# A graph network on one core: counts of two target rows kept in one float32 value, and two layers that unpack them and multiply exact parts in single-pass products, a block at a time

## The reference, cut to what matters

```python
def _L0_gnn_ref(feature, edge_src, edge_dst, W1, b1, W2, b2):
    msgs = feature[edge_src]
    neigh = jax.ops.segment_sum(msgs, edge_dst, num_segments=N_NODES)
    h = (1.0 + EPS) * feature + neigh
    h = jax.nn.relu(h @ W1 + b1)
    return h @ W2 + b2
...
def _L2_gnn_ref(x, edge_index, w_self, b_self, w_neigh, b_neigh):
    agg = jax.ops.segment_sum(x[src], dst, num_segments=n)
    deg = jnp.maximum(deg, 1.0)[:, None]
    mean_neigh = agg / deg
    return x @ w_self.T + b_self + mean_neigh @ w_neigh.T + b_neigh
...
h = relu(layernorm(x)); x = x + _L0_gnn_ref(h, src, dst, ...)
h = relu(layernorm(x)); x = x + _L1_gnn_ref(h, edge_attr_64, ...)   # attention over edges
h = relu(layernorm(x)); x = x + _L2_gnn_ref(h, edge_index, ...)
h = relu(layernorm(x)); x = x + _L3_gnn_ref(h, src, dst, edge_weight, ...)
```

## Time and profile before

| | |
|---|---|
| median of 3 timed runs | 5309.13 us (5304.78 to 5313.57) |
| profiled execution, its own time | 5340.31 us |
| its span in the trace | 5338.3 us |
| mean granted PE clock | 0.927 |
| busy: PE, DVE, ACT, POOL | 4369.5, 3074.2, 1790.3, 2045.5 us |

### The profile page before, as it was taken

The page is one execution under the profiler, slowest core; times in us unless marked ns, Lnnn a source line. Parts: engine busy times, 40 slices in busy tenths (PEclk is TensorE's granted clock), DMA queues, the critical chain, the costliest instruction groups (busy, mean ns, idle before and its releaser), DMA issues. The chain is left out here.

```text
span 5338.3 us, 89156 instructions
## 1 busy us (share of the span) xinstructions
PE 4369.5 (82%) x26128; PEld 3033.2 (57%) x26129; DVE 3074.2 (58%) x4341; ACT 1790.3 (34%) x3211; POOL 2045.5 (38%) x1963
## 2 busy tenths in 40 slices
PE   4776666667999868888888888888883599999999
PEld 3443322225888635555555555555552488888888
DVE  3319887774111288999999899899985600000000
ACT  3562578893000210122333444455552300001000
POOL 3420353000000057777777777777772400000000
PEclk8899988888999989999999999999995699999999
DMA  8774667557666443445555556666665566669998
GB/s 183 200 216 116 230 267 281 238 250 304 267 271 288 163 124 101 129 140 151 153 167 173 174 183 196 186 187 202 199 206 167 198 280 274 274 263 289 299 299 261
DMA packets 594565, 1140.92 MB, mean 214 GB/s; under 512 B 106507, under 2 KB 518497, under 8 KB 575612
## 3 DMA queue, kind: packets, MB, share of 16 engines
q1 hardware_dynamic: 414223, 675.37, 36.5%
q10 hardware_dynamic: 117215, 327.75, 16.3%
q0 software_dynamic: 63024, 136.64, 10.4%
HBM read 760.37 MB, written 389.00 MB: 215 GB/s over the span
## 5 line engine op out<-in xcount | busy, mean ns | idle before, releaser
L1613 POOL DMA_INDIRECT at_qg<-q_d,at_slot x1616 | 1644.0, 1017 | 495.6 <-issue 492.2
L807 PE MATMUL bw_ps<-bw_mov,bw_sta 128*128 128x392 bf16 x7056 | 1590.8, 349 | 17.3 <-issue 6.9
L1155 PE MATMUL at_p3t<-tiles,h 128*128 128x256 f32 (+1 forms) x4900 | 1047.9, 375 | 5.7 <-ACT h L1010 5.4
L1155 PEld LDWEIGHTS at_p3t<-tiles,h 128*128 128x128 f32 x4900 | 913.7, 190 | 126.5 <-issue 5.9
L1656 PE MATMUL at_psk<-at_kp,at_hot 128*128 x4848 | 618.9, 235 | 319.2 <-DVE at_qg L1734 269.9
L807 PEld LDWEIGHTS bw_ps<-bw_mov,bw_sta 128*128 128x128 bf16 x7056 | 639.6, 102 | 365.6 <-issue 98.0
L1656 PEld LDWEIGHTS at_psk<-at_kp,at_hot 128*128 128x128 bf16 x4848 | 441.2, 101 | 665.4 <-issue 461.5
L807 PE MATMUL ba_ps<-ba_mov,ba_sta 128*128 128x392 bf16 x2352 | 521.9, 369 | 315.8 <-ACT ba_ps L766 126.7
L770 DVE TENSOR_TENSOR ba_mov<-iota,key 128x3136 bf16<-128x3136 f16 x294 | 525.9, 1789 | 135.4 <-PE ba_ps L807 130.3
L807 PEld LDWEIGHTS ba_ps<-ba_mov,ba_sta 128*128 128x128 bf16 x2352 | 244.2, 104 | 593.1 <-issue 479.9
L791 DVE TENSOR_TENSOR bw_sta<-bw_raw,kw 128x1024 bf16<-128x1024 bf16 x882 | 557.2, 686 | 0.0
(11 more groups left out here) (434 smaller groups left out, 3272.1 us busy)
## 6 DMA issues: line engine op xcount, KB each, us to landing
adj_d<-ba_stage ACTq DMA_DIRECT2D x49, 3136.0 KB, 8.9
l0adjt<-adj_d SPq DMA_DIRECT2D x23, 6272.0 KB
tiles<-adw_d SPq DMA_DIRECT2D x23, 6272.0 KB, 20.4
tiles<-adj_d SPq DMA_DIRECT2D x22, 6272.0 KB, 17.4
adw_d<-xall ACTq DMA_DIRECT2D x65, 1568.0 KB
adw_d<-bw_stage ACTq DMA_DIRECT2D x33, 1568.0 KB
at_rel<-rel_d SPq DMA_DIRECT2D x101, 512.0 KB
et_attr<-in_edge_attr SPq DMA_DIRECT2D x48, 1024.0 KB
```

The source lines that it names most:

```text
L807: ins = pe.matmul(self.ps[:, bass.DynSlice(place, WCOL)], self.sta[:, k, u // 2, :, u % 2], self.mov[:, u // 2, :, u % 2], start=False, st ...
L1155: ins = pe.matmul(ps_agg[par][:, 0:n * P], h[:, hi, :], moving[hi], start=hi == 0, stop=hi == NB - 1 and not own_term, skip_group_check=ow ...
L1613: pool.indirect_dma_start(out=qg[:, ring, b, :], out_offset=None, in_=q_d[:, :], in_offset=bass.IndirectOffsetOnAxis(ap=slot[:, ring, b:b ...
```

## The change

- **Two counts in one value.** A window has 16 target rows. An edge of the lower 8 adds 1 to its place, one of the upper 8 adds 2^-12 (`LOW`) to the same place. `ba_mov` is therefore made by one two-operation pass a visit: equal to the key, times the scale. Windows fall from 784 to 400 and visits from 2352 to 1968. A block of counts is 1.6 MB instead of 3.1.
- **Paged rows.** Every 15 chunks of edges begin a page and the row numbers go up by one, so that a node's edges may lie in two rows and no count overflows its 12 bits. There are 50 blocks of such rows. A small matrix (`rows_of`) merges the paged rows into the node rows after the product.
- **Tables.** The windows by 16 paged rows are for the counts; those by 8 node rows are kept for the weighted build. Each needs its passes over tails and visits and its gathers (16 and 19).
- **Layers one and three** run in `CountLayer`, one block at a time: SP loads it, DVE splits it into the two counts in two passes (`unpack`), PE multiplies the block of counts, as stationary operand and in the type float32r, by 256 columns: the high and the low part of the rows of `h`, which `Split` makes so that products are exact. ACT and DVE add the two halves of the sum, PE merges rows, and the same small products follow for 128 columns.
- **Moved.** The gate goes from DVE in the first layer to POOL in the count stage, behind the gathers. The places of ends go to the count stage.
- The last layer has its own function, with the same work.

```diff
--- before.py
+++ after.py
+PAGE = 15
+PAGES = -(-NCH // PAGE)
+PAGE_SCALE, PAGE_SHIFT = 4370, 16
+assert all(k * PAGE_SCALE >> PAGE_SHIFT == k // PAGE for k in range(CROWS)) and P * PAGE < 1 << 11
+BOUNDS = PAGES - 1
+NBV = -(-(N + BOUNDS) // P)
+NPADV = NBV * P
+VR = 2 * WN
+WPBV = P // VR
+NWV = NPADV // VR
+NVISV = NCH + NWV
+VGV = -(-NVISV // P)
+LAST = NPADV - 1 - BOUNDS
+HALF = P // 2
+LOW = 2.0 ** -12
...
+        tails_below(NBV, True)
+        visits, regs_v = visits_of(by_rows)
...
+        tails_below(NB, False)
+        chain(ve.tensor_copy(full[:], ps[:, 0, 0:NB]))
+        visits, regs = visits_of(by_nodes)
...
+            looked = chain(ve.scalar_tensor_tensor(out=k, in0=k, scalar=1.0, in1=o, op0=ALU.add, op1=ALU.mult))
+            wait(pe, looked)
+            b0, t0 = turn(k, GV)
+            b1, t1 = turn(l, GV)
+            read(c.key, i0, GV, b0, t0, -1.0)
+            b2, t2 = turn(dq, GV)
+            before.append(t2)
+            read(c.lo, i0, GV, b1, t1, 0.0)
+            read(c.scale, i0, GV, b2, t2, LOW, scale=1.0 - LOW)
...
+        ve.wait_ge(x.s_bounds, 16)
+        chain(ve.tensor_tensor(x.bound_i[:], x.bound_i[:], x.part_i[:, 0:1], ALU.add))
+        chain(ve.tensor_scalar(x.bound_i[:], x.bound_i[:], 1, None, ALU.add))
+        chain(ve.tensor_scalar(bounds_i[:, 0:1], x.bound_i[:], P - 1, None, ALU.bitwise_and), ve.tensor_scalar(bounds_i[:, 1:2], x.bound_i[:], 7, None, ALU.arith_shift_right))
+        chain(ve.tensor_copy(bounds[:, 0:2], bounds_i[:]))
+        m = chain(ve.tensor_scalar(bover[:], vrow[:], bounds[:, 0:1], None, ALU.is_ge), ve.tensor_scalar(bhere[:, 0, :], c.iota[:, 0:NBV], bounds[:, 1:2], None, ALU.is_equal),
+                  ve.tensor_scalar(bhere[:, 1, :], c.iota[:, 0:NBV], bounds[:, 1:2], None, ALU.is_gt))
+        wait(pe, m)
...
-    def one_hots(self, out, keys, width):
-        return self.nc.vector.tensor_tensor(out, self.iota[:, 0:width, :].unsqueeze(1).to_broadcast([P, UV // 2, width, 2]), pairs(keys).unsqueeze(2).to_broadcast([P, UV // 2, width, 2]), ALU.is_equal)
...
-        self.one_hots(self.mov[:, v, :, :], c.key[:, bass.DynSlice(t, UV)], WCOL)
-        self.one_hots(self.sta[:, 0, v, :, :], c.lo[:, bass.DynSlice(t, UV)], P).then_inc(self.s_hot, UV)
...
+        for u in range(UV):
+            ve.tensor_scalar(self.mov[:, u0 + u, :], c.iota, c.key[:, bass.DynSlice(t + u, 1)], c.scale[:, bass.DynSlice(t + u, 1)], ALU.is_equal, ALU.mult)
+        pairs_of_one_hots(ve, self.sta[:, u0 // 2:(u0 + UV) // 2, :, :], c.iota2, c.lo[:, bass.DynSlice(t, UV)], P).then_inc(self.s_hot, UV)
...
+        Gate(nc, c, lambda n, shape: ctx.enter_context(nc.sbuf_tensor(n, shape, F32))).run()
         ring = 3 * UV
-        b = Build(nc, c, ctx, False, ring)
+        b = CountBuild(nc, c, ctx, ring)
...
-        with nc.vector.Fori(0, NVIS // ring) as i:
+        with nc.vector.Fori(0, NVISV // ring) as i:
...
+class Split:
+    def __init__(self, nc, c, room, parts):
+        self.nc, self.c, self.parts, self.q = nc, c, parts, c.steps
+        h, high = (room[:, k * 2 * 7 * D:(k + 1) * 2 * 7 * D].rearrange("p (t k d) -> p t k d", t=2, d=D) for k in range(2))
+        self.h, self.high = h, high.bitcast(I32)
+    def rows(self, t):
+        act, norm, q = self.nc.scalar, self.c.norm, self.q
+        q.low.wait(act, t - 1)
+        for k in range(7):
+            b = 7 * t + k
+            act.activation(self.h[:, t % 2, k, :], self.c.x[:, b, :], ACT.Relu, bias=norm.nbias[:, b:b + 1], scale=norm.rstd[:, b:b + 1]).then_inc(norm.s_rows, 1)
+    def parts_of(self, t):
+        ve, q = self.nc.vector, self.q
+        h, high = self.h[:, t % 2, :, :], self.high[:, t % 2, :, :]
+        ve.wait_ge(self.c.norm.s_rows, 7 * (t + 1))
+        q.high.wait(ve, t - 1)
+        wait(ve, self.c.V(ve.tensor_scalar(high, h.bitcast(I32), -(1 << 12), None, ALU.bitwise_and)))
+        q.low.inc(ve.tensor_tensor(self.parts[:, 7 * t:7 * (t + 1), 1, :], h, high.bitcast(F32), ALU.subtract))
+    def keep_high(self, t):
+        pool, q = self.nc.gpsimd, self.q
+        q.low.wait(pool, t + 1)
+        q.high.inc(pool.tensor_copy(self.parts[:, 7 * t:7 * (t + 1), 0, :], self.high[:, t % 2, :, :].bitcast(F32)))
...
+    def load(self, i, k, lap):
+        sp, q = self.nc.sync, self.q
+        q.cast.wait(sp, i - RAW + 1)
+        q.raw[k % RAW].inc(sp.dma_start(self.raw[k % RAW].rearrange("p h n -> p (h n)"), self.c.adj_d[bass.DynSlice(i, 1), :, :].rearrange("a p n -> (a p) n")), 16)
+    def unpack(self, i, k, lap):
+        ve, q = self.nc.vector, self.q
+        raw, cast = self.raw[k % RAW], self.cast[k % 2]
+        q.raw[k % RAW].wait(ve, 16 * (lap + k // RAW) + 16)
+        q.product.wait(ve, i - 1)
+        q.odd.inc(ve.tensor_scalar(cast[:, :, HALF:P], raw, ROUND, -ROUND, ALU.add, ALU.add))
+        q.odd.wait(ve, i + 1)
+        q.cast.inc(ve.tensor_tensor(cast[:, :, 0:HALF], raw, cast[:, :, HALF:P].bitcast(F32), ALU.subtract))
+    def sum_parts(self, i, k):
+        ve, q = self.nc.vector, self.q
+        q.product.wait(ve, i + 1)
+        q.merged.wait(ve, i - 1)
+        q.low_sum.wait(ve, i + 1)
+        q.summed.inc(ve.tensor_tensor(self.agg[:, k % 2, :], self.ps_acc[k % 2][:, 0:D], self.low_sum[:, k % 2, :], ALU.add))
+    def low_part(self, i, k):
+        act, q = self.nc.scalar, self.q
+        q.product.wait(act, i + 1)
+        q.summed.wait(act, i - 1)
+        q.low_sum.inc(act.copy(self.low_sum[:, k % 2, :], self.ps_acc[k % 2][:, D:2 * D]))
+    def rows_of(self, i, k):
+        pool, q, c = self.nc.gpsimd, self.q, self.c
+        q.merged.wait(pool, i - 1)
+        at = self.at[:, k % 2:k % 2 + 1]
+        q.place.inc(pool.tensor_copy(at, c.row_in_block[:, bass.DynSlice(i, 1)]))
+        q.place.wait(pool, i + 1)
+        pool.sem_inc(q.go, 1)
+        q.rows.inc(pool.tensor_scalar(self.rows[:, k % 2, :], c.iota[:, 0:2 * P], at, c.row_scale[:, 0:1], ALU.is_equal, ALU.mult))
+    def own_rows(self, r, k):
+        pool, q = self.nc.gpsimd, self.q
+        self.e.own_used(self, pool, r)
+        own = self.parts[:, bass.DynSlice(r, 1), :, :].rearrange("p a t d -> p (a t) d").bitcast(F32)
+        q.own.inc(pool.tensor_tensor(self.own[:, k % 2, :], own[:, 0, :], own[:, 1, :], ALU.add))
+    def product(self, i, k, first=False):
+        pe, q = self.nc.tensor, self.q
+        q.cast.wait(pe, i + 1)
+        q.summed.wait(pe, i - 1)
+        for hi in range(NB):
+            if first and hi % 7 == 0:
+                q.high.wait(pe, hi // 7 + 1)
+            ins = pe.matmul(self.ps_acc[k % 2][:, 0:2 * D], self.cast[k % 2][:, hi, :], self.parts[:, hi, :, :].rearrange("p t d -> p (t d)"), start=hi == 0, stop=hi == NB - 1)
+        q.product.inc(ins)
+    def merge(self, i, k):
+        pe, q = self.nc.tensor, self.q
+        q.summed.wait(pe, i + 1)
+        q.rows.wait(pe, i + 1)
+        agg, rows, opened, closed = self.agg[:, k % 2, :], self.rows[:, k % 2, :], self.ps_sum[k % 2], self.ps_sum[(k + 1) % 2]
+        if here(i, NB):
+            q.aggT.wait(pe, i - 1)
+            if self.e.self_term:
+                q.own.wait(pe, i + 1)
+                pe.matmul(opened[:, 0:P], self.own[:, k % 2, :], self.c.ident[:], start=True, stop=False, skip_group_check=True)
+            ins = pe.matmul(opened[:, 0:P], agg, rows[:, P:2 * P], start=not self.e.self_term, stop=False, skip_group_check=True)
+        if here(i - 1, NB):
+            ins = pe.matmul(closed[:, 0:P], agg, rows[:, 0:P], start=False, stop=True, skip_group_check=True)
+        q.merged.inc(ins)
+    def turned_sum(self, r, k):
+        act, q = self.nc.scalar, self.q
+        q.merged.wait(act, r + 2)
+        self.e.sum_used(self, act, r)
+        q.aggT.inc(act.copy(self.aggT[:, k % 2, :], self.ps_sum[k % 2][:, 0:P]))
+    def update(self, r, k):
+        ve, q, c = self.nc.vector, self.q, self.c
+        q.out.wait(ve, r + 1)
+        self.e.update(self, r, k)
+        q.updated.wait(ve, r + 1)
+        c.norm.block_stats(c.x, r)
...
+    def pe(self):
+        def body(i, k, lap):
+            if here(i, NBV):
+                self.product(i, k, first=isinstance(i, int) and i == 0)
+            if here(i - 1, NBV):
+                self.merge(i - 1, k - 1)
+            if here(i - 3, NB):
+                self.e.middle(self, i - 3, k - 3)
+            if here(i - 4, NB):
+                self.e.output(self, i - 4, k - 4)
+        in_steps(self.nc.tensor, body, NB + 4)
+    def act(self):
+        def body(i, k, lap):
+            if here(i, NBV):
+                self.low_part(i, k)
+            if here(i - 2, NB):
+                self.turned_sum(i - 2, k - 2)
+            if here(i - 3, NB):
+                self.e.read_middle(self, i - 3, k - 3)
+        in_steps(self.nc.scalar, body, NB + 3)
+    def ve(self, biased):
+        def body(i, k, lap):
+            if here(i + 1, NBV):
+                self.unpack(i + 1, (k + 1) % STEADY, lap + (k + 1) // STEADY * (STEADY // RAW))
```

(15 more changed lines are left out.)

1057 lines of the change are left out of this document (594 added, 463 removed).

## The result

The changed kernel takes 5162.67 us (median of 4 runs, 5147.14 to 5168.31) where the kernel before took 5308.66 beside it: a ratio of 0.9711 [0.9695, 0.9726], 146 us faster. The prediction was 4870 with a range of 4770 to 5060, so the sign is right and the size missed by twice the gain that came. The profiled execution took 5147.14 against a forecast of 4901: 246 are to be found. Every ratio in this document compares the undisturbed (fast) executions of two kernels alone, so it can rest on fewer executions than the median beside it; where few are left, the text says so.

What follows compares the result with a forecast made beforehand. PE was taken to bound both layers, with DVE near its limit in the count build. Terms +24 - 166 - 165 - 135 + 3 = -439 took the profiled 5340.3 to 4901, timed 4870, range 4770 to 5060.

Steps and rivals of the forecast that it cites:

- The cover: Count stage: POOL has nothing else to do, so the gate's 35 us behind the gathers are hidden by the build.
- the build's pace: Count build on DVE: a pass 0.24 us, a group 2.7, 246 groups, 674 us against 840, so -166.
- Rival 6: Count stage: POOL becomes a bound beside a busy DVE, stage 50 to 90 us longer, 4925 to 4960; chance 0.08.
- Rival 2: Count build: the short compare passes are not cheap, 0.34 us each, time 5036; chance 0.17.
- Index tables: Stage before the count build: second pass over tails and visits delays the start, +24 us, bounds +10 and +50.
- First layer: First layer: DVE becomes the bound at 7.6 us a block, 424 us against 589, so -165.
- Third layer: Third layer: as the first, 7.94 us a block on DVE, -135; bias pass on POOL 5.4 us.
- Rivals 4 and 5: Both layers, PE: a product takes 0.218 us (5270) or 0.435 (6335, slower than before); chance 0.06 each.
- rival 3: Both layers, DVE: the rounding pass is fast, 1.84 us, leaving DVE under PE's 6.7 a block, 4780; chance 0.13.

## Why the prediction was wrong

**The step that failed** is in the count stage: "it has nothing else to do in this stage, so 35 us are hidden behind the build; without that cover they would cost themselves". The cover was computed from POOL's idle time alone, as though POOL's work and DVE's went side by side. Measured in its place: gathers of 279 and 245 us, and a wait of 190 behind the build, of which 107 are gathers and 82 the gate. The experiments show from both sides that DVE's stream holds the gathers. In the six kernels whose stream has breaks, no gather lasts over 1.71 us. Of the six profiled executions of a stream without breaks in which gathers could run, five have one of 245 to 748 us. The gate wasn't covered either. Beside the build it costs DVE 65 of its 85 us, so that even where no gather was held (the change on the third chip) the stage took 814 us and not 674: 60 for the build's pace, 71 for the gate and the gathers, 10 behind the build. And its price was off: 35 us in the prediction, 82 to 85 in the runs.

**What the step left unread.** The gathers' 1838 ns beside the build against 0.94 ahead of it already said that the two engines exclude each other. That isn't the work of DVE's pauses: 64 of the 101 gathers of the kernel before stand beside a DVE without a gap, and they take 2.01 us on the mean and 2.53 at most. One of them, with DVE's operations around it:

```profile
599.72 2.00 POOL L905 DMA_INDIRECT tv_rows<-ed_d,tv_place  x1 [0.30 <-issue]
599.12 1.78 DVE L770 TENSOR_TENSOR ba_mov<-iota,key 128x3136 bf16<-128x3136 f16 x1
600.82 0.69 DVE L770 TENSOR_TENSOR ba_sta<-iota,lo 128x1024 bf16<-128x1024 f16 x1
601.42 1.78 DVE L770 TENSOR_TENSOR ba_mov<-iota,key 128x3136 bf16<-128x3136 f16 x1
```

It ends 0.82 after the long comparison does (600.90), so it got its turn where one operation follows the other, without a pause. In the change the same gather waits past hundreds of such places. Breaks in the stream are enough to end that; why it begins is open.

**Rival 6** had this mechanism ("beside a DVE that works all the time its operations are stretched") at 0.08 and 50 to 90 us. It was priced as a stretching by a factor; in fact one instruction can be held for hundreds of microseconds. Of the page cited there (the Trainium skill, "GPSIMD Engine Reference", section 1), the direction was right. It says that the contention is with a two-port mode or with two inputs, and it gives no bound. The layers' rows agree with both kinds: POOL waits for the quick one-input pass and for the two-input subtraction, and not for the slow one-input pass. The stream of two-input operations alone (530.38) agrees with the second kind. Rival 6 priced it at 50 to 90 us: 71 came where no gather was held, and a wait of 190 where two were. The page's 2.2 ns an element, by which I had put the gate at an estimated 65 us, is nearer than my 0.86 from the copies: the gate's addition (L1214) takes 3.48 us at 1568 elements, 2.2 ns each as the page has it, its largest group (L1217) 4265 ns, 2.7 each, and the gate took 82.

**The build's pace.** A pass was to be 0.24 and a group 2.7; measured 0.29 to 0.30 and 2.94, +60 us. The estimate of 0.13 as fixed part of a short pass was too low: taking 0.11 of streaming off the 0.29 to 0.30 leaves 0.18 to 0.19, near the 0.20 that I had read off the short row and then cut. Rival 2's 0.34 was as near as my 0.24; by its own figures, 846 against 674, it was worth 172 us and not 166. It isn't the register step (0.29 without it). PE and ACT are no limit, as foreseen: DVE has no wait in the stream.

**Index tables**: +33, within the bounds of +10 to +50.

**First layer**: right, point by point. Period 7.61 for 7.6, the rounding pass 3.41 for 3.46, subtraction pitch 3.42 for 3.35, product 0.125 for 0.113 without effect since DVE was the bound, and 429 for 424. **Third layer**: period 8.0 to 8.4 for 7.94, 424 for 410 us; its bias pass on POOL took 13.59 us for 5.4, as the copies' rate was too low here too. (The 7.94 is 7.6 with the operation of 0.346 added, as the kernel has it, and not in place of a small one.) Rivals 4 and 5, that the product isn't a single pass, are excluded by the 6.11 for 49; rival 3 by the 3.41.

**Luck.** On the third chip the same kernel came to 0.950 of the kernel before, and the upper end of the range, 5060, is 0.953 of the 5309 before. Had the change been timed there first, the forecast would have looked nearly right, with the cover still wrong: in the execution that was profiled the gathers got through, and the gate stretched the build. The attention stage's 37 us, for which the prediction has nothing, also brought the result nearer to it.

**What stays open.** The same kernel ran its gathers unhindered in one profiled execution (the third chip) and not in another, and in the second a gather passes in 2.62 us and the next, started at the same point of DVE's group, stands for 244.77. The long gather of 407 us on the second chip and those of 496, 530 and 748 on the first say that being held is common, not certain, and I found no row that decides it. Up to the gathers the streams are alike (groups of 2.94 in both), and where the gathers get through, two of them pass to each group, which is then 3.05. What holds a gather, as against an elementwise operation of POOL, is told apart in part: DVE's operations with two inputs do so by themselves (530.38), the statistics passes don't, and no run has the 392-wide pass alone. That DVE's wait in attention is scatter is argued from other executions, not shown.

**The better version** that came out of this is the kernel with breaks in 22 rounds, the gate on DVE in the index stage and the split at 48 rows: 0.928 of the kernel before, where the change had 0.950 on the same chip. Stage by stage there: 771 against 814 in the count stage, 402 against 430 in the first layer, 375 against 426 in the third.

## What to carry to other kernels

Before work is hidden on POOL behind DVE, compare the same POOL instruction's duration inside and outside of DVE's stream (here 1.84 and 0.94 us): if they differ, POOL's idle time is no cover, and the loss may be far larger than the difference. Where POOL's result is needed soon, give DVE's stream planned breaks (0.33 us for a group here), or put POOL's work where DVE isn't yet streaming: the gate cost 82 us behind the build, 65 beside it and at most 13 ahead of it. One good execution doesn't clear such a kernel, since the same kernel had its gathers held in one and not in another. And of an odd number of rows, split off one: here that was worth 28 and 51 us in two layers for one added line.

## What the runs showed of the hardware that was not expected

- A gather on POOL, 0.95 us when alone, stood for 245 to 748 us beside a DVE stream without a gap in five profiled executions, and in one for at most 1.49. In four of the five the last held one ended 0.83 us after the last one-hot pass, while DVE went straight on with statistics passes of one input. With a pause of 0.24 us at each group it took 1.05 on the mean.
- An unbroken stream of two-input comparisons, in the kernel before, let 64 gathers pass in 2.01 us on the mean; an unbroken stream of two comparisons and a multiplication held one for 530.
- An elementwise operation of POOL waits for the end of a quick one-input pass (0.18 becomes 1.60) and of a two-input one (0.46 becomes 2.95), and runs at its own length beside a slow one-input pass (0.45 to 0.48).
- In the other direction, elementwise work on POOL stretched a group of DVE's from 3 us to 10 to 20, and gathers back to back did as well; one gather in a pause added 0.02.
- Eight compares of 392 elements with two pointers go at 0.29 to 0.30 us each, with the pointer's address from a register or fixed; with a source at a step of two, 0.39.
- A float32 pass over 49 rows of 64, whose rows stand 128 apart on the output side, takes 3.41 us, over 48 rows 1.75.
- A single-pass float32 product of 128x128 by 128x256 goes at 0.125 us with its weight load beside it, in a stretch whose mean granted clock is 0.95 of the 2.4 GHz level.
